# Position tables of an attention layer as one stationary square, made two items ahead, and a reordering of three engines' queues

## The chip, the cores and the metric

One core of a Trainium2 chip runs the whole kernel. The metric is the device time of one execution in microseconds (us). A profiled execution also gives its span, the time from its first to its last instruction.

## The reference

Four layers on x of shape 4 x 16 x 16 x 1024 (1024 tokens, 1024 channels), each behind a group norm (32 groups, over tokens and channels) and with a residual sum:

```python
x = x + L0(gn(x))   # lambda layer: q, k, v projections, position table, 4 heads
x = x + L1(gn(x))   # masked attention, 16 heads of 64, then Wo
x = x + L2(gn(x))   # attention, 16 heads of 64, biases, position tables, then a projection
x = x + L3(gn(x))   # 3x3 filter, tensor-train channel product (4 cores), bias, relu

# L2, for one image (H = W = 16) and one head of 64 channels
attn = (q * scale) @ k.T
rel_h = einsum('bhwc,hkc->bhwk', q, rel_pos_h[h - k + H - 1])
rel_w = einsum('bhwc,wkc->bhwk', q, rel_pos_w[w - k + W - 1])
attn = softmax(attn + rel_h[..., :, None] + rel_w[..., None, :])
out = attn @ v
```

## The kernel before

Channels lie on the partitions, tokens on the free axis. The five engines run queues written out by hand, tied together by semaphores; SyncE and ScalarE issue the DMAs. Every large product is made in three matmuls, since both operands are split into a rounded head (hi) and a rest (lo): hi x hi, lo x hi and hi x lo, summed in one bank of PSUM. Weights come from DRAM in slots of 4 chunks of 128 rows (w_load on SyncE), and GpSimd splits each (w_split, lines 226 and 228); three slots go round.

**Items.** Layers 1 and 2 are cut into 4 stages of 8 items (ITEMS = 32, PAIRS = 8). Stage s holds one layer (s = 0, 1: layer 1; 2, 3: layer 2) for one half of the tokens, two images; item i is one pair of heads, j = i % 8. Items 16 to 31 are layer 2's. With the last item of a stage done, 8 out blocks of 24 matmuls make the output projection (in item 8, 16, 24 for the stage before).

**TensorE's queue** in item i (attention_pe): scores(i) (line 1182), relative(i + 1) (line 1234), project K(i + 1), Q(i + 2) and V(i), 24 matmuls each (line 1138), attend(i - 1) (lines 1203, 1214). In items with j = 0 attend(i - 1) stands ahead of V(i), and the out blocks follow. Item 30 has K(31), V(30), attend(29), scores(31). The end mixes the halves of the last out blocks with V(31), attend(30), attend(31) and then with build_m, 16 pairs of matmuls that make the matrix M of layer 3; their heads are copied by ScalarE (line 1754), their rests by VectorE (line 1759), over two banks. last_pe (line 1786) waits for all of M.

**Position tables.** relative makes, per query and head, the products with all 31 entries of both tables: 24 matmuls with the queries stationary and 64 columns of table moving, into half a bank each of REL = (7, 0). Bank 7 is also Q's, bank 0 also V's, so relative waits for v_turned, that is turn_values (line 1497) on VectorE. ScalarE copies the result to SBUF in two parts (evac_relative, line 1387) and issues one DMA to DRAM (line 1624); SyncE reads it back with 8 DMAs whose skewed pattern picks each query's own entries (strips_from_dram, line 1636), and VectorE adds row and column part (sum_relative, line 1530).

**Softmax.** Per item 4 steps k: VectorE adds the tables and takes the maximum (lines 1470, 1473), ScalarE makes exponentials with their sum (line 1353), VectorE inverts (line 1488), ScalarE normalises (line 1363), VectorE turns 32x32 squares (line 1484). The turned probabilities and values go through DRAM; ScalarE copies the values (take_v, line 1344). ScalarE copies heads of Q, K and O (lines 1373/1377, 1396/1398, 1408/1410), VectorE makes their rests (1504/1506, 1513/1515, 1536/1539).

**Group norm of the next stage.** VectorE adds each out block to x (lines 1547, 1549), takes statistics (373), aggregates (379) and makes group moments (328 to 337), GpSimd the power (388), VectorE coefficients (342, 393). In items j = 1 to 4, chunk pairs are normalised: y on both engines (408, 406), head on ScalarE (414), rest on VectorE (419).

## Time and profile before

| | |
|---|---|
| times of the kernel before | 1235.68 us median of 3 (1235.05 to 1236.21) |
| the profiled execution | 1237.92 us, its span 1236.1 us |
| TensorE matmuls busy | 1198.9 us (97%) |
| VectorE, GpSimd, ScalarE busy | 697.4 (56%), 641.8 (52%), 475.7 (38%) |
| mean granted clock of TensorE | 0.99 of full speed |
| DMA | 171.81 MB, mean 139 GB/s |
| chain that ended last | TensorE 80%, VectorE 9%, issue 4%, ScalarE 3%, DMA 3% |

The busy time is the union of an engine's rows; matmuls overlap in their ends, so a mean duration of one (some 390 ns) is longer than the distance of two. Distances and counts tell the pace. The chain of waits is followed back from the last instruction to what released each step; a piece of it with "x72" is 72 instructions on end. Idle time of an engine that holds up nobody costs nothing.

### The profile page before, as it was taken

What the parts mean: (1) busy time and instruction counts of PE and PEld (TensorE: products, weight loads), DVE (VectorE), ACT (ScalarE), POOL (GpSimd) and SP (SyncE); (2) the same over time, 40 slices, a digit from 0 to 9 for tenths busy, and PEclk for the clock granted to TensorE, in tenths of its full rate; (3) what the DMA queues carried; (4) which work ended last, traced back from release to release, by engine and by line L of the source; (5) the groups of instructions that cost most, each with busy time, mean ns of one, the idle gap of its engine ahead of it and who ended that gap; (6) DMA issues with size and microseconds to landing.
All of it is one profiled execution on the core that took longest, in us unless ns stands there. A gap on an engine that the chain in (4) does not pass through costs nothing.

```text
span 1236.1 us, 19275 instructions
## 1 busy us (share of the span) xinstructions
PE 1198.9 (97%) x6640; PEld 970.9 (79%) x6640; DVE 697.4 (56%) x1434; ACT 475.7 (38%) x1229; POOL 641.8 (52%) x726
## 2 busy tenths in 40 slices
PE   6999999999999999999999999999998999999998
PEld 4788896478888888888878878788787878777887
DVE  7534443775665433765552577867337787458312
ACT  3611241035655410755540154545105545343312
POOL 4633389346556566656556645555564655463000
PEclk9999999999999999999999989999998999999999
DMA  5211114025666753576665357868535677720012
GB/s 186 84 44 51 35 52 122 8 65 178 189 187 180 208 167 95 151 206 178 198 181 158 96 157 211 237 197 242 174 103 161 176 209 229 208 97 1 34 35 68
DMA packets 159136, 171.81 MB, mean 139 GB/s; under 512 B 30656, under 2 KB 110176, under 8 KB 159040
## 3 DMA queue, kind: packets, MB, share of 16 engines
q1 hardware_dynamic: 148736, 163.70, 45.2%
q10 hardware_dynamic: 10304, 6.88, 1.8%
q8 instruction: 53, 0.87, 0.3%
q14 instruction: 43, 0.35, 0.1%
HBM read 120.20 MB, written 46.14 MB: 135 GB/s over the span
## 4 chain that ended last, share of the span: by engine, by line
PE 80%; DVE 9%; issue 4%; ACT 3%; DMA 3%; POOL 1%; SPq 1%; ACTq 0%; DVEq 0%; POOLq 0%
PE PS L1138 47%; PE PS L1786 7%; PE PS L682 7%; PE PS L962 3%; PE PS L1182 3%; PE PS L971 2%; PE PS L977 2%; PE PS L1214 2%; PE PS L1803 2%; PE PS L665 1%; PE PS L1203 1%; PE PS L1234 1%; DVE PS L1470 1%; DVE part L1530 1%; DVE bst L257 1%
## 5 line engine op out<-in xcount | busy, mean ns | idle before, releaser
L1138 PE MATMUL PS<-XB,w_hi 128*128 128x512 f32 x1024 | 334.6, 396 | 1.8 <-POOL w_lo L228 1.2
L226 POOL CAST w_hi<-w_raw 128x512 fp32r<-128x512 f32 x195 | 124.6, 639 | 298.6 <-PE PS L1138 214.8
L228 POOL TENSOR_TENSOR w_lo<-w_raw,w_hi 128x512 fp32r<-128x512 f32 x195 | 256.8, 1317 | 15.6
L1138 PEld LDWEIGHTS PS<-XB,w_hi 128*128 128x128 f32 x1024 | 194.0, 190 | 45.7 <-issue 3.2
L1353 ACT ACTIVATE part<-PS,nmax 128x256 f32<-128x256 f32 (+1 forms) x256 | 112.4, 444 | 290.7 <-DVE nmax L1473 182.4
L1138 PE MATMUL PS<-XB,w_lo 128*128 128x512 f32 x512 | 201.1, 393 | 0.0
L1138 PE MATMUL PS<-XB,part 128*128 128x512 f32 x768 | 189.0, 395 | 0.6 <-ACT part L1387 0.6
L1138 PEld LDWEIGHTS PS<-XB,part 128*128 128x128 f32 x768 | 145.5, 191 | 31.5 <-issue 1.0
L1484 DVE STREAM_TRANSPOSE part<-part 128x384 f32<-128x384 f32 (+1 forms) x128 | 82.1, 641 | 70.2 <-ACT part L1363 68.5
L1363 ACT ACTIVATE part<-part,prec 128x256 f32<-128x256 f32 (+1 forms) x256 | 105.9, 474 | 35.3 <-DVE prec L1488 27.2
L228 POOL TENSOR_TENSOR part<-part,part 128x512 fp32r<-128x512 f32 x85 | 111.2, 1309 | 6.8
L1138 PEld LDWEIGHTS PS<-XB,w_lo 128*128 128x128 f32 x512 | 97.1, 190 | 19.6 <-issue 0.2
L1138 PE MATMUL PS<-part,w_hi 128*128 128x512 f32 x344 | 111.0, 391 | 0.2 <-POOL w_lo L228 0.2
L226 POOL CAST part<-part 128x512 fp32r<-128x512 f32 x85 | 53.8, 633 | 102.5 <-PE PS L1138 95.6
L1138 PEld LDWEIGHTS PS<-part,w_hi 128*128 128x128 f32 x344 | 64.6, 188 | 14.6 <-issue 1.1
L682 PE MATMUL PS<-XB,w_hi 128*128 128x512 f32 x256 | 70.9, 392 | 0.0
L1138 PE MATMUL PS<-part,w_lo 128*128 128x512 f32 x172 | 66.9, 389 | 0.0
L1530 DVE TENSOR_TENSOR part<-part 128x512 f32<-128x512 f32 x64 | 61.2, 975 | 0.3 <-DMA part<-strips 0.3
L1138 PE MATMUL PS<-part,part 128*128 128x512 f32 x252 | 60.6, 389 | 0.0
L598 DVE COPY part<-PS 64x512 f32<-64x512 f32 x32 | 34.6, 1080 | 44.2 <-PE PS L700 43.9
L682 PEld LDWEIGHTS PS<-XB,w_hi 128*128 128x128 f32 x256 | 47.4, 188 | 9.4
L1138 PEld LDWEIGHTS PS<-part,part 128*128 128x128 f32 x252 | 47.1, 188 | 9.7
(135 smaller groups left out, 1800.7 us busy)
## 6 DMA issues: line engine op xcount, KB each, us to landing
w_raw<-in_w SPq DMA_DIRECT2D x187, 256.0 KB, 2.8
part<-in_w SPq DMA_DIRECT2D x85, 256.0 KB, 3.0
part<-turned SPq DMA_DIRECT2D x32, 512.0 KB, 5.5
turned<-part SPq DMA_DIRECT2D x60, 256.0 KB, 4.4
turned<-part SPq DMA_DIRECT2D x64, 192.0 KB, 3.4
part<-turned SPq DMA_DIRECT2D x32, 384.0 KB, 4.4
values<-part SPq DMA_DIRECT2D x128, 64.0 KB, 2.3
part<-values SPq DMA_DIRECT2D x32, 256.0 KB, 4.7
```

What stands on the lines that cost most here:

```text
L226: pool.tensor_copy(hi, raw).then_inc(w_hi_done, 1)
L228: pool.tensor_tensor(lo, raw, hi.bitcast(F32), ALU.subtract).then_inc(w_ready, 1)
L598: last = nc.vector.tensor_copy(dst, src)
L682: m = nc.tensor.matmul(PS[:, 2 * (n % 2) + h, :], wt[:, (c % 4) * P:(c % 4) * P + P], x_part(hl, h, c), start=c == k == 0, stop=c == CK - ...
L962: m = nc.tensor.matmul(bank[0:rows * SIDE, (x - x0) * w:(x - x0) * w + w], table, Qs[:, jp, x * N + SIDE * y0:x * N + SIDE * y1], start=jp ...
L1138: m = nc.tensor.matmul(PS[:, bank, :], wt[:, (c % 4) * P:(c % 4) * P + P], rhs(hl, c), start=c == k == 0, stop=c == CK - 1 and k == 2)
L1182: m = nc.tensor.matmul(PS[:, S + 2 * a + hh, at + lo:at + hi], x[rows, qs], y[rows, cols], start=k == 0, stop=k == 2)
L1353: last = nc.scalar.activation(prob[:, n % 2, at:at + hi - lo], PS[:, S + k, qt * N + lo:qt * N + hi], ACT.Exp, bias=nmax[:, k, qt:qt + 1], ...
L1363: last = nc.scalar.activation(p, p, ACT.Copy, scale=prec[:, k, qt:qt + 1])
L1484: nc.vector.transpose(dst, src).then_inc(t_done, 1)
L1530: nc.vector.tensor_tensor(both_rel[:, n % 2, :, :, :], of_row, of_col, ALU.add).then_inc(rel_sum, 1)
L1786: m = nc.tensor.matmul(PS[:, bank, :], x3(hl, b, c, tt * P), w[:, c, half * HALF:half * HALF + HALF], start=c == k == 0, stop=c == CK - 1 ...
```

## The change

- The tables' product has the table as the stationary square (2 tables x 2 heads x 32 rows, 128x128) and all 512 queries moving, reordered to image column, image and row: 3 matmuls into bank 7. It is made for item i + 2, behind the fifth chunk of V(i) (values_block).
- Its result is turned by one VectorE transpose of 32x32 squares (turn_relative), and ScalarE issues four DMAs for it at the end of its item. The reading pattern follows the new order.
- In layer 2, evac_q and rest_of_q of item i + 2 stand ahead of the last normalisation and the last turn.
- take_v stands ahead of the last exponentials in items with j = 0 and in item 30.
- Norm: statistics and aggregation of each out block right behind its sum; group moments at the end of item j = 1, coefficients in j = 2, chunks in j = 2 to 5; the rest is made by GpSimd. rest_of_o stands two steps later.
- The first half of out block 6 stands ahead of attend(31); M goes over four banks.

```diff
-            for o in {ITEMS - 2: (0,), ITEMS - 1: (1, 2, 3, 4, 5)}.get(i, ()):
+            for o in {ITEMS - 2: (0,), ITEMS - 1: (1, 2, 3, 4, 5, 6)}.get(i, ()):
...
-            take((3, "O", o), 2, "O", o, (1,) if o < 6 else range(2))
+            take((3, "O", o), 2, "O", o, (1,) if o < 7 else range(2))
...
-            def rest(self, t, c):
-                nc.vector.wait_ge(self.y_dve, CK * t + c + 1)
-                nc.vector.wait_ge(self.hi, CK * t + c + 1)
-                nc.vector.tensor_tensor(self.out(t, 1, c), self.ytmp[:, c % 2, :], self.out(t, 0, c).bitcast(F32),
-                                        ALU.subtract).then_inc(self.lo, 1)
+            def rest(self, eng, t, c):
+                eng.wait_ge(self.y_dve, CK * t + c + 1)
+                eng.wait_ge(self.hi, CK * t + c + 1)
+                eng.tensor_tensor(self.out(t, 1, c), self.ytmp[:, c % 2, :], self.out(t, 0, c).bitcast(F32),
+                                  ALU.subtract).then_inc(self.lo, 1)
...
-    all_rel = carve(19456, [P, 4, 2, 2, 32])
+    all_rel = carve(19456, [P, HALF])
...
-    REL = (X, 0)
...
-    LAST_OUT = (1, X, S, S + 1, S + 2, 0)
+    LAST_OUT = (1, X, S, S + 1, S + 2, 0, S + 3, S + 2)
...
     def out_bank(s, o):
-        return LAST_OUT[o % 6] if s == 3 else (O, 0)[o % 2]
...
-    M_AFTER = {(0, 1): (0, 1), (1, 1): (2, 3), (2, 1): (4,), (3, 1): (5, 6), (4, 1): (7, 8), (5, 1): (9,),
-               (6, 0): (10, 11), (6, 1): (12, 13), (7, 0): (14, 15), (7, 1): ()}
-    M_BANKS = (S + 3, O)
+        return LAST_OUT[o] if s == 3 else (O, 0)[o % 2]
...
+    M_AFTER = {(0, 1): (0,), (1, 1): (1,), (2, 1): (2,), (3, 1): (3, 4), (4, 1): (5, 6, 7), (5, 1): (8, 9),
+               (6, 1): (10, 11, 12), (7, 0): (13, 14, 15), (7, 1): ()}
+    M_BANKS = (O, 1, X, S)
...
-                        pe.wait_ge(rel_evac, 2 * (i - 1 - LO_KEYS) + 2)
+                        pe.wait_ge(rel_evac, i - LO_KEYS)
...
-                    if LO_KEYS <= i + 1 < ITEMS:
-                        pe.wait_ge(rel_evac, 2 * (i + 1 - LO_KEYS) + 2)
...
         def relative(i):
...
-            if i == ITEMS or layer_of(i) == 1:
...
+            if i >= ITEMS or layer_of(i) == 1:
...
-            pe.wait_ge(v_turned, i - 1)
-            if i % PAIRS == 2:
-                pe.wait_ge(sum_done, CK * (i // PAIRS))
...
-            for tt in range(4):
-                for k, (x, y) in enumerate(((qh[i % 2], rel_hi), (qh[i % 2], rel_lo), (ql[i % 2], rel_hi))):
-                    for hh in range(2):
-                        rows = slice(64 * hh, 64 * hh + 64)
-                        to = PS[:, REL[hh], 64 * tt:64 * tt + 64].rearrange("p (t n) -> p t n", t=2)
-                        m = nc.tensor.matmul(to, x[rows, tt * P:tt * P + P], y[rows, :, 32 * hh:32 * hh + 32],
-                                             start=k == 0, stop=k == 2)
-                        if (tt, k) == (3, 2):
-                            m.then_inc(rel_done, 1)
+            for k, (x, y) in enumerate(((rel_hi, qh[i % 2]), (rel_lo, qh[i % 2]), (rel_hi, ql[i % 2]))):
+                m = nc.tensor.matmul(PS[:, X, :], x.rearrange("p r n -> p (r n)"), y.rearrange("p (a y x) -> p y a x", a=2, y=SIDE),
+                                     start=k == 0, stop=k == 2)
+            m.then_inc(rel_done, 1)
...
         def out_block(s, o, chunks):
...
-                beside = 6 if s == 3 else 2
-                if c == 0 and o >= beside:
-                    pe.wait_ge(sum_done, CK * s + o - beside + 1)
+                if c == 0 and s < 3 and o >= 2:
+                    pe.wait_ge(sum_done, CK * s + o - 1)
+                if c == 0 and s == 3 and o == 7:
+                    pe.wait_ge(sum_done, CK * s + 5)
...
-                    pe.wait_ge(rel_evac, 2 * (ITEMS - LO_KEYS))
-                if s == 3 and c == 0 and 2 <= o < 5:
-                    pe.wait_ge(p_exp, 4 * LAST + o - 1)
+                    pe.wait_ge(rel_evac, ITEMS - LO_KEYS)
+                if s == 3 and c == 0 and out_bank(s, o) in range(S, S + 4) and o < 7:
+                    pe.wait_ge(p_exp, 4 * LAST + out_bank(s, o) - S + 1)
...
         def build_m(i):
...
-            if i == 1:
+            if i == 0:
...
-            if i >= 2:
-                pe.wait_ge(m_lo, i - 1)
+            if 1 <= i < 4:
+                pe.wait_ge(sum_done, 3 * CK + i)
+            if i >= 4:
+                pe.wait_ge(m_lo, i - 3)
...
         def score_block(i):
...
-            relative(i + 1)
...
+        def values_block(i):
...
+            project(i, "V", range(0, 5))
+            relative(i + 2)
+            project(i, "V", range(5, CK))
...
-                project(i, "V", range(CK))
+                values_block(i)
...
-                project(i, "V", range(CK))
+                values_block(i)
...
-        for o in (3, 4, 5):
+        for o in (3, 4, 5, 6):
...
-        for o in range(6):
-            out_block(3, o, range(4, CK))
-            for k in M_AFTER[o, 1]:
-                build_m(k)
-        for o in range(6, CK):
-            for half in range(2):
+        for o in range(CK):
+            for half in range(0 if o == 7 else 1, 2):
...
-                if i > LO_KEYS:
-                    act.wait_ge(rel_done, 2 * (i - LO_KEYS) - 2)
+                if i > LO_KEYS + 1:
+                    act.wait_ge(rel_done, i - LO_KEYS - 1)
...
-        def evac_relative(i):
-            if i == ITEMS or layer_of(i) == 1:
-                return
-            if i > LO_KEYS:
-                act.wait_ge(strips_out, 16 * (i - LO_KEYS))
-            for hh in range(2):
-                act.wait_ge(rel_done, 2 * (i - LO_KEYS) + hh + 1)
-                nc.scalar.activation(all_rel[:, :, :, hh, :],
-                                     PS[:, REL[hh], 0:4 * 64].rearrange("p (t a n) -> p t a n", t=4, a=2), ACT.Copy).then_inc(rel_evac, 1)
-            strips_to_dram(act, i)
...
-            evac_relative(i + 1)
...
-            if i == LAST:
+            early = i and j == 0 or i >= LAST - 1
+            if early:
...
+            if layer_of(i) == 2:
+                evac_q(i + 2)
...
-            if 0 < i < LAST:
+            if i and not early:
...
-            if 1 <= j <= 4:
-                for c in (2 * j - 2, 2 * j - 1):
+            if 2 <= j <= 5:
+                for c in (2 * j - 4, 2 * j - 3):
...
-                for c in (2 * j - 2, 2 * j - 1):
+                for c in (2 * j - 4, 2 * j - 3):
...
-            evac_q(i + 2)
+            if layer_of(i) == 1:
+                evac_q(i + 2)
...
+            if LO_KEYS <= i + 2 < ITEMS:
+                strips_to_dram(act, i + 2)
...
+        def turn_relative(i):
...
+            if i >= ITEMS or layer_of(i) == 1:
+                return
+            dve.wait_ge(rel_done, i - LO_KEYS + 1)
+            if i > LO_KEYS:
+                dve.wait_ge(strips_out, 64 * (i - LO_KEYS))
+            nc.vector.transpose(all_rel, PS[:, X, :]).then_inc(rel_evac, 1)
...
-        norm.group_stats(1)
...
-            if i >= 2 and j != 1:
-                rest_of_o(i - 2)
...
+            if i >= 2 and j != 1:
+                rest_of_o(i - 2)
...
+            if layer_of(i) == 2:
+                rest_of_q(i + 2)
...
-            if j == 1:
+            if j == 2:
...
-            if 1 <= j <= 4:
-                for c in (2 * j - 2, 2 * j - 1):
+            if 2 <= j <= 5:
+                for c in (2 * j - 4, 2 * j - 3):
...
-                for c in (2 * j - 2, 2 * j - 1):
-                    norm.rest(s + 1, c)
-            rest_of_q(i + 2)
+            if layer_of(i) == 1:
+                rest_of_q(i + 2)
...
-            sum_relative(i + 1, 1)
+            turn_relative(i + 2)
...
+            sum_relative(i + 1, 1)
...
-                    if o:
-                        stats_of(s - 1, o - 1)
-                stats_of(s - 1, CK - 1)
-                norm.aggregate(s + 1, range(CK), 16)
+                    stats_of(s - 1, o)
+                    norm.aggregate(s + 1, (o,), 2 * o + 2)
+            if j == 1:
...
-            if o >= 6:
+            if o == 7:
...
-                for k in (2 * o - 12, 2 * o - 11):
-                    stats_of(3, k)
...
-        for o in range(4, CK):
+            if o in (1, 2):
+                stats_of(3, o - 1)
+        for o in range(2, CK):
...
     def strips_to_dram(sp, i):
...
-        sp.wait_ge(rel_evac, 2 * done + 2)
-        whole = strips[buf].rearrange("(t p) n -> p t n", p=P)
-        sp.dma_start(whole, all_rel[:, :, :, :, :].rearrange("p t a b n -> p t (a b n)")).then_inc(strips_out, 16)
+        sp.wait_ge(rel_evac, done + 1)
+        rows = strips[buf].rearrange("(ax y) n -> ax y n", y=SIDE)
+        for b in range(4):
+            src = all_rel[32 * b:32 * b + 32, :].rearrange("p (y n) -> p y n", y=SIDE)
+            sp.dma_start(rows[:, :, 32 * b:32 * b + 32], src).then_inc(strips_out, 16)
...
     def strips_from_dram(sp, i):
...
-        sp.wait_ge(strips_out, 16 * (done + 1))
+        sp.wait_ge(strips_out, 64 * (done + 1))
...
-            at = buf * HALF * P + tt * P * P + 15
-            for k, first, steps in ((0, at - 8 * (tt % 2), (SIDE * P - 1, P)), (1, at + 64, (SIDE * P, P - 1))):
+            at = (buf * HALF + SIDE * SIDE * (tt // 2) + 8 * (tt % 2)) * P + 15
+            for k, first, steps in ((0, at - 8 * (tt % 2), (P - 1, SIDE * P)), (1, at + 64, (P, SIDE * P - 1))):
...
+            if n == PROBS_AT[LAST] + 2:
+                values_from_dram(sp, LAST)
...
-                values_from_dram(sp, LAST)
-            if n == PROBS_AT[LAST] + 2:
...
     def attention_pool(pool):
...
-                if n == (slots[(PAIRS * s + 3, "Q"), 0] if s else slots[(2, "Q"), 0]):
+                if n == slots[(PAIRS * s + 2, "K"), 0] + 8:
...
-            if n == slots[(ITEMS - 1, "Q"), 0]:
+                for j in range(2, 6):
+                    if n == slots[(PAIRS * s + j + 1, "K"), 0] + 8:
+                        for c in (2 * j - 4, 2 * j - 3):
+                            norm.rest(nc.gpsimd, s + 1, c)
+            if n == slots[(ITEMS - 1, "V"), 0]:
...
-            if n == slots[(3, "O", 3), 1]:
+            if n == slots[(3, "O", 6), 1]:
...
-            if n == slots[(3, "O", 5), 1]:
+            if n == slots[(3, "O", 7), 0]:
...
```

## Rows read from the trace of the kernel before

**Rows 1.** The chain of waits, one item of layer 2: start us, us, what.
```profile
832.88 1.62 PE PS L1182 x24
834.50 1.26 PE PS L1234 x24
835.76 16.52 PE PS L1138 x72
852.28 1.88 PE PS L1203 x16
```

**Rows 2.** TensorE's timeline: start, us, line, operation, [idle before, released by].
```profile
722.51 2.42 PE L1234 MATMUL PS<-part,part 64*128 64x64 f32 x24 [2.50 <-DVE part L1497]
...
791.65 1.53 PE L1234 MATMUL PS<-part,part 64*128 64x64 f32 x24 [1.70 <-DVE part L1497]
...
930.63 2.97 PE L1138 MATMUL PS<-XB,part 128*128 128x512 f32 x12 [0.59 <-ACT part L1387]
...
994.77 1.68 PE L1234 MATMUL PS<-part,part 64*128 64x64 f32 x24 [0.96 <-DVE part L1497]
```

**Rows 3.** Busy time of each engine, granted clock, DMA share by stretches.
```profile
696.30:743.70 47.40, 44.38 (x257) 36.10 (x256) 38.46 (x84) 24.39 (x67) 24.39 (x25) 0.93 0.50 139
...
1086.40:1121.50 35.10, 32.99 (x154) 26.40 (x152) 26.48 (x29) 19.00 (x17) 18.40 (x18) 1.00 0.15 46
```

**Rows 4.** The chain of waits, the projections behind two late tables blocks.
```profile
724.93 18.84 PE PS L1138 x72
...
996.45 17.92 PE PS L1138 x72
```

**Rows 5.** Timeline of TensorE and ScalarE, late attention products and a copy.
```profile
870.33 1.95 PE L1203 MATMUL PS<-part,part 128*64 128x256 f32 x16 [2.21 <-issue]
...
1053.70 3.42 PE L1203 MATMUL PS<-part,part 128*64 128x256 f32 x16 [2.21 <-issue]
...
869.62 0.62 ACT L1344 ACTIVATE part<-part 128x512 f32<-128x512 f32 x1
```

**Rows 6.** TensorE's timeline, the last attention product.
```profile
1085.39 1.08 PE L1203 MATMUL PS<-part,part 128*64 128x256 f32 x8 [0.85 <-DMA part<-turned]
```

**Rows 7.** The chain of waits, matmuls of layer 0.
```profile
196.92 20.60 PE PS L971 x48
217.52 6.87 PE PS L977 x16
```

**Rows 8.** Timeline of ScalarE and VectorE in the item of rows 1.
```profile
838.01 0.66 ACT L1387 ACTIVATE part<-PS 128x256 f32<-128x256 f32 x2
...
846.46 0.20 ACT L1353 ACTIVATION_READ_ACCUMULATOR part<-PS,nmax 128x1 f32 x1
...
849.57 0.75 DVE L1506 SCALAR_TENSOR_TENSOR part<-PS,bias,part 128x512 fp32r<-128x512 f32 x1 [0.33 <-ACT part L1377]
...
852.54 0.70 DVE L1497 STREAM_TRANSPOSE part<-PS 128x512 f32<-128x512 f32 x1
```

**Rows 9.** DMA of 832.88:854.16 and 846.2:849.9, stretch, SyncE's issue.
```profile
q10 hardware_dynamic: 528, 0.26, 4.1%
part<-values SPq DMA_DIRECT2D x1, 256.0 KB, 5.3
...
q1 hardware_dynamic: 861, 0.16, 21.2%
...
832.88:854.16 21.28, 21.28 (x138) 17.34 (x138) 15.34 (x24) 10.53 (x30) 12.49 (x13) 1.00 0.79 237
...
860.31 0.48 SPq L1672 DMA_DIRECT2D part<-values  x1
```

**Rows 10.** The page's costliest groups, a line's rows, GpSimd's timeline.
```profile
L228 POOL TENSOR_TENSOR w_lo<-w_raw,w_hi 128x512 fp32r<-128x512 f32 x195 | 256.8, 1317 | 15.6
...
L419 DVE TENSOR_TENSOR XB<-part,XB x40: 676/693/1765, 246.1 to 1012.0; 128x512 fp32r<-128x512 f32 x40
...
838.82 0.61 POOL L226 CAST part<-part 128x512 fp32r<-128x512 f32 x1 [5.04 <-PE PS L1138]
```

10 lines of the change are left out of this document (5 added, 5 removed).

## The prediction, made before the run

> **What bounds the kernel now.** I read the shares of busy time first: TensorE is busy for 97% of the span (table above), no other engine for more than 56%. So a microsecond counts only if TensorE's own row loses it: work taken off TensorE, or a pause of it. Next I read the chain of waits in a quiet item of layer 2 [rows 1]. Scores 1.62, position tables 1.26, three projections 16.52 and the attention product 1.88 follow each other without a pause, 21.28 us in all. The reader is to see that nothing but TensorE sets this item. I call the end of its scores T0 (834.50).
>
> Then I listed TensorE's rows that carry an idle time. Four tables blocks of layer 2 wait for VectorE's line 1497 (turn_values, which frees bank 0 of REL): 2.50, 1.70 and 0.96 us here, 2.50 once more at 947.76 [rows 2]. After such a wait the same work is slower: the mean granted clock of the stretch from 696 to 744 is 0.93 [rows 3], and the 72 projections behind take 18.84 and 17.92 us in place of 16.52 [rows 4]. A part of them runs at the lower level, 1.2 GHz, the rest at 2.4. Three attention products, at 870.33, at 1053.70 and a like one at 643.97, come 2.21 us late, marked "issue"; ScalarE's take_v (869.62 for 0.62 us) ends 0.1 us before the first of them starts, so that copy is the releaser [rows 5]. The last product waits 0.85 us for a DMA [rows 6].
>
> **The position tables.** Removed: 24 matmuls of 64 columns per item, 1.26 us [rows 1]. Added: 3 of 128x512. At 229 ns (16.52/72) they are 0.69 us; 16 items x 0.57 = 9.1 us. Their moving operand is read in runs of 16 elements, which no full-rate row here does. Lines 971 and 977 move 512 columns, one in runs of 4 elements and one contiguously, and both take 429 ns a matmul (20.60/48, 6.87/16) [rows 7]. So scattered reading is free there, and I take 229 ns. The bound the other way is 429 ns, 1.29 us per item and no gain: 9 us. A gain beyond 0.57 is excluded, since 229 ns is the fastest 512-column row.
>
> ScalarE loses two copies (line 1387, 838.01 for 0.66 us, with the issue behind it 1.1), VectorE gains one transpose like line 1497's, 0.70 us [rows 8]. It stands where VectorE would next wait for V, so the wait covers it; without that cover 0.70 would come off the 1.9 us of slack below.
>
> **Their place.** The block moves behind the fifth chunk of V and an item further ahead. It no longer waits for turn_values, since bank 0 is not used. What goes [rows 2, 4], against the quiet item: 2.50 + (2.42 - 1.26) + (18.84 - 16.52) = 5.98, twice; 0.96 + 0.42 + 1.40 = 2.78; 1.70 + 0.27 = 1.97. With the waits for line 1387 (0.59, and a like one of 0.52 at 705.37) that is 17.8 us. What is late next is the queries' rest (q_lo): the block stands 11.0 + 15 x 0.229 = 14.5 us after T0, and behind it the rest of V, the attention product and the next scores are queued. Before, line 1506 ended at 850.32, T0 + 15.8 [rows 8]: too late by 1.3. The change puts ScalarE's copy right behind the last exponential and VectorE's rest ahead of the last turn. That exponential ends at 846.66, T0 + 12.2 [rows 8]; without line 1387 ahead of it some 1.1 earlier, T0 + 11.1, just as the queries' product is done. Copy 0.67, rest 0.75: ready at T0 + 12.6, slack 1.9 us. After the out blocks VectorE today starts late because statistics and group moments stand ahead of the maxima; they are spread or moved behind the next item, so it starts about 1 us late, inside the slack. In the layer 1 items 14 and 15 no sum of tables stands ahead, and the old order already gives about T0 + 12.7.
>
> **DMAs of the move.** ScalarE issues 4 DMAs per item instead of 1, after turn_relative (about T0 + 17 to 19): about 0.5 us each by SyncE's issue in [rows 9], twice that if the queues are full (an estimate), 2 to 4 us. Queued behind them are evac_o and the next exponentials, due at about T0 + 21.5. So they are covered at the low end, and the high end takes some of the next item's slack. The bytes are the same but come in 2048 pieces of 128 bytes, against 528 packets now. These 528 took 4.1% of 16 engines over 21.28 us, 26 ns each; the strip reads of 192 bytes 14.6 ns (21.2% of 16 x 3.7 us / 861) [rows 9]. Between those prices the engines get 1.0 to 2.5 us more work each per item, on a share of 0.79 [rows 9]: 0.86 to 0.93. I take the lower, nearer in size. Weight loads have two slots of slack, so TensorE should not see it; the item in which it might is below. The page "DMA: Bandwidth & Descriptors" of the Trainium skill (Specifications) says that transfers below 512 bytes do a read-modify-write and miss line rate. That speaks against these pieces; 26 ns would then be no upper bound. The 192-byte rows here are reads, so no run shows it yet.
>
> **Take_v early.** In items 16, 24 and 30 the values' copy moves ahead of the last exponential. Gone: 3 x 2.21, and behind the last one 3.42 - 1.88 = 1.54 of slower products: 8.1 us [rows 1, 5]; 3.42 against 1.88 is near the ratio of the two levels. The copy needs the values in SBUF: issued at 860.31 (T0 of that item 855.78, so T0 + 4.5) and, at the 5.3 us that the like load took an item before, landing at T0 + 9.8 [rows 9], while the product can start at T0 + 11.0. The margin is 0.6 us after the copy. A load 2 us later would give back 1.4 each, 4 us.
>
> **Normalisation.** Two subtractions per item for four items of each stage go from VectorE to GpSimd (1.32 us each by its other subtractions, line 228). They stand in GpSimd's long pause during attention and scores (5.04 us before 838.82) [rows 10], so they cost nothing; without that pause 2.6 us would come off the some 3 us by which a split weight is ahead of its use. VectorE's subtraction takes 0.68 at least and up to 1.77 [rows 10]. The page "SBUF — State Buffer" (Who interferes with whom) says that a VectorE instruction with two SBUF inputs contends with a GpSimd one that reads SBUF, and one fully waits; by it two more GpSimd reads may hold VectorE for up to 2.6 us per such item and eat the 1.9 of slack. The spread of rows 10 agrees that there is something of the kind.
>
> **The end.** One more half block ahead of the last attention product covers its wait, 0.85 us [rows 6]; four banks instead of two for the M products, with their waits of about 0.5 each, are worth 1.3 us: after the last attention the phase took 35.1 us [rows 3], and laying products and copies out by hand gives 33.8, with TensorE waiting 1.8 us for VectorE's last copy. It may be worth nothing. Together 2.1. Charged: the last scores now come at T0 + 12.9 and need the keys' rest at T0 + 13.5, 0.6 us; item 30's product comes some 5 us sooner, its values' load only 3 to 4: 1.0 us.
>
> **Sum.** 9.1 + 17.8 + 8.1 + 2.1 - 1.6 = 35.5. The profiled execution took 1237.92 (span 1236.1), the median of the runs is 1235.68, 2.24 less; the saving applies to either. 1235.68 - 35.5 = 1200.2, so 1200.
>
> **Rivals.** (1) *Part is given back*: tables matmuls at 429 ns (9 us), or values that land late under the small pieces (4 to 8 us). For: no row shows either in its new form; against: [rows 7], and the margin of 0.6. 1209. (2) *The pauses after the out blocks stay*, as VectorE is still late there and another of its results is next; 12 us back: 1212, or 1217 with the other two. For: VectorE starts those items late today [rows 2]; against: the next result in line, the keys' rest, is made at about T0 + 14.5 and due at T0 + 19.1. (3) *Slower*: the queries' rest misses T0 + 14.5 in every item, so the block waits in the middle of V. A wait of 0.96 cost 2.78 and one of 2.50 cost 5.98 [rows 2, 4], as the clock falls too; 14 items at 2.5 us each eat the gain, which is decided at about 0.9 us beyond the slack. At the old place of line 1506 (1.3 late, some 3.5 each) it would be 1200 + 49 = 1249. Against: the two moves of this change. (4) *The change doesn't do what it says*: the waits move one for one, 1235.
>
> **Chances.** Forecast 0.62, with its own range 1192 to 1206; rival 1 0.20; rival 2 0.10; rival 3 0.06; rival 4 0.02. 1190 to 1214 leaves out rivals 3 and 4, the far end of 2 and a little of the forecast. About 0.2% is what a measurement of this kernel can tell from no change. Faster 0.92, same 0.02, slower 0.06.
>
> **What would show it.** Right: a steady item of 20.7 us; a tables block of 3 matmuls in about 0.7 us with no idle ahead; no row "issue 2.21" before attention; the granted clock 1.00 in the items after the out blocks. Wrong: idle before the tables block released by q_lo (rival 3); a block of 1.3 us (rival 1); VectorE as releaser of other TensorE rows after the out blocks (rival 2); line 1344 waiting for a DMA in items 16 and 24.

## The result, and the profile after

The changed kernel takes 1201.9 us (median of 4 runs, 1201.2 to 1204.8) against 1236.0 for the kernel before on the same chip: ratio 0.972, 95% interval 0.969 to 0.975. The forecast was 1200, with a range of 1190 to 1214. Unaltered and run five times more on another chip it gave 1202.9 (0.971, 0.969 to 0.974). The nine runs together have a median of 1202.2; "the changed kernel" is that number below. The profiled execution took 1204.8, span 1202.8.

The page of the kernel after: busy time by engine, then packets and queues.

```profile
PE 1178.2 (98%) x6304; PEld 949.5 (79%) x6304; DVE 674.2 (56%) x1418; ACT 462.9 (38%) x1197; POOL 683.4 (57%) x758
...
DMA packets 184478, 171.78 MB, mean 143 GB/s; under 512 B 64192, under 2 KB 135520, under 8 KB 184384
...
q10 hardware_dynamic: 35648, 6.89, 3.0%
```

TensorE is still the bound. The packets under 512 bytes have doubled (30,656 before), while ScalarE's queue, q10, takes 3.0% of the engines' time.

The chain of waits of the kernel after, a quiet item (start, us, what), which answers [rows 1]:

```profile
712.66 1.62 PE PS L1179 x24
714.28 14.50 PE PS L1137 x63
728.78 0.72 PE PS L1227 x3
729.50 2.06 PE PS L1137 x9
731.57 1.88 PE PS L1200 x16
733.45 1.62 PE PS L1179 x23
```

One item is 20.79 us against 21.28. The tables block is 0.72 in place of 1.26, and V in its two parts takes 0.04 more. The block stands in the middle of V with nothing idle ahead of it.

The same kernel by windows (length, then busy us of each engine, granted clock, DMA share, GB/s): the stretch that answers the first of [rows 3], and the phase of the M products behind the last attention.

```profile
691.87:733.45 41.58, 41.58 (x233) 33.11 (x232) 33.51 (x65) 21.18 (x59) 26.79 (x27) 1.00 0.61 172
1056.50:1088.16 31.66, 30.25 (x142) 24.90 (x140) 25.52 (x29) 18.27 (x17) 17.91 (x17) 0.97 0.15 42
```

The clock is 1.00 where it was 0.93. What is left of TensorE's pauses is this (timeline of PE from 600 us on, its rows with an idle time; in brackets the idle time ahead and what ended it):

```profile
851.66 1.95 PE L1200 MATMUL PS<-part,part 128*64 128x256 f32 x16 [1.56 <-issue]
1023.04 1.70 PE L1179 MATMUL PS<-part,part 64*128 64x256 f32 x24 [0.96 <-DVE part L1504]
1038.96 1.30 PE L1200 MATMUL PS<-part,part 128*64 128x256 f32 x10 [0.40 <-issue]
1054.88 1.69 PE L1200 MATMUL PS<-part,part 128*64 128x256 f32 x8 [1.84 <-DMA part<-turned]
1083.78 0.50 PE L1267 MATMUL PS<-ttA,part 96*128 96x256 f32 x2 [0.28 <-DVE part L1763]
1088.16 2.11 PE L1790 MATMUL PS<-part,XB 128*128 128x512 f32 x8 [1.13 <-DVE part L1763]
```

Every wait of [rows 2] is gone. Of the three of [rows 5], those of items 16 and 30 are gone and 1.56 of item 24's 2.21 is left. Three stand near the end: the keys' rest ahead of scores(31) (0.96), the values ahead of attend(30) (0.40) and the last probabilities ahead of attend(31, 1) (1.84, before 0.85 [rows 6]).

The starts of the scores say where the 33.3 us between the two profiled spans lie: 24.4 in items 17 to 23 and 25 to 29, 4.3 in item 16, 1.2 in item 24, 4.0 in item 30 and 0.2 before all these, less 0.7 behind scores(31).

ScalarE's and VectorE's timeline in another quiet item, whose scores end (T0) at 818.21:

```profile
829.35 0.69 ACT L1372 ACTIVATE part<-PS,bias 128x512 fp32r<-128x512 f32 x1 [1.37 <-PE PS L1137]
...
830.08 0.75 DVE L1495 SCALAR_TENSOR_TENSOR part<-PS,bias,part 128x512 fp32r<-128x512 f32 x1 [1.90 <-ACT part L1372]
```

The queries' rest is ready at 830.83, T0 + 12.6; the block starts at T0 + 14.3. Both are as forecast. The total, the item and this step agree, and so it looked as if the whole sum were right. The experiments say that it isn't.

### The profile page after: what moved, and what is told of

Same layout as the page of the kernel before. It is cut to its first block, busy times and chain, and to the rows that moved or that the text cites. A ratio compares the mean times of both kernels' runs of the same rounds, so it can differ in the third digit from the quotient of the medians.

```text
span 1202.8 us, 18617 instructions
## 1 busy us (share of the span) xinstructions
PE 1178.2 (98%) x6304; PEld 949.5 (79%) x6304; DVE 674.2 (56%) x1418; ACT 462.9 (38%) x1197; POOL 683.4 (57%) x758
## 4 chain that ended last, share of the span: by engine, by line
PE 91%; DVE 4%; DMA 2%; issue 1%; SPq 1%; POOL 1%; ACT 0%; ACTq 0%; POOLq 0%; DVEq 0%
PE PS L1137 55%; PE PS L1790 7%; PE PS L682 7%; PE PS L1179 4%; PE PS L962 3%; PE PS L971 2%; PE PS L977 2%; PE PS L1200 2%; PE PS L1211 2%; PE PS L1807 2%; PE PS L665 1%; DVE part L1763 1%; PE PS L1227 1%; DVE bst L257 1%; PE PS L700 1%
## 5 line engine op out<-in xcount | busy, mean ns | idle before, releaser
L1179 PE MATMUL PS<-part,part 64*128 64x256 f32 (+1 forms) x768 | 53.0, 284 | 1.0 <-DVE part L1504 1.0
```

Source lines behind the costliest of these rows:

```text
L1179: m = nc.tensor.matmul(PS[:, S + 2 * a + hh, at + lo:at + hi], x[rows, qs], y[rows, cols], start=k == 0, stop=k == 2)
```

## The experiments

Times are medians; the difference is to the changed kernel's 1202.2. The number in brackets is the ratio to the kernel before, measured beside it on the same chip, with its 95% interval.

### Which part brought what: four kernels between before and after

The first undoes the whole of the tables and leaves the rest of the change. (REL is bank X and bank 0 again; relative(), evac_relative() and the strips' layout are those of the kernel before.)

```
         def score_block(i):
             scores(i, 0)
             scores(i, 1)
+            relative(i + 1)
...
-            project(i, "V", range(0, 5))
-            relative(i + 2)
-            project(i, "V", range(5, CK))
+            project(i, "V", range(CK))
...
-            if layer_of(i) == 2:
-                evac_q(i + 2)
             normalize(i, 3)
```

> The changed kernel with the whole of the tables undone: 24 matmuls of 64 columns one item ahead behind the scores, two ScalarE copies, one DMA of the strips, the queries' copy and rest late. Everything else of the change stays (statistics and moments spread, the normalisation's rests on GpSimd, take_v early, four banks for M, the order at the end). Prediction's sum: tables 9.1 + their place 17.8 = 26.9 slower than the changed kernel, 1229. Rival: the spread statistics and moments alone let VectorE's turn_values come sooner behind the out blocks, so the waits of 2.50, 1.70 and 0.96 are gone without a new place, and the tables are worth only 9 to 15 us: 1211 to 1217.

Measured: 1209.0 (0.977, 0.974 to 0.979), 6.8 slower, not 27. On TensorE's timeline no tables block waits for turn_values any more, although the block is at its old place, in its old banks and behind the same wait. The block of item 18 follows its scores at once, where [rows 2] have 2.50 us:

```profile
713.28 1.69 PE L1182 MATMUL PS<-part,part 64*128 64x256 f32 x24
714.81 1.42 PE L1234 MATMUL PS<-part,part 64*128 64x64 f32 x24
```

The rival came true, and below its own low end. Next, the statistics alone are undone, once with the new tables and once with the old ones.

```
-            if j == 2:
+            if j == 1:
                 norm.coefficients(s + 1)
-            if 2 <= j <= 5:
-                for c in (2 * j - 4, 2 * j - 3):
+            if 1 <= j <= 4:
+                for c in (2 * j - 2, 2 * j - 1):
...
                     add_out(s - 1, o)
-                    stats_of(s - 1, o)
-                    norm.aggregate(s + 1, (o,), 2 * o + 2)
-            if j == 1:
+                    if o:
+                        stats_of(s - 1, o - 1)
+                stats_of(s - 1, CK - 1)
+                norm.aggregate(s + 1, range(CK), 16)
                 norm.group_stats(s + 1)
```

> The changed kernel with the statistics undone: after each stage's out blocks VectorE makes the statistics in one row behind the sums, with the group moments ahead of the next item's maxima, and the next normalisation stands in items 1 to 4 of a stage, not 2 to 5. Tables stay as changed. If two remedies are each enough for the waits of 2.50, 1.70 and 0.96 us (the tables' new bank and place, and VectorE's lighter item), the waits stay away here too: at most 3 us slower than the changed kernel, 1202 to 1206. If the light items are needed: VectorE comes some 2 us later into the queries' rest of item 17 and 25, past the 1.9 us of slack, and the tables block waits there: 5 to 12 us slower.

> The kernel with both undone: tables, their place and the queries' copies as before, statistics and normalisation as before; kept are only the rests on GpSimd, the rest of the attention output and the last sum of tables one step later in VectorE's row, take_v early, four banks for M and the order at the end. If the statistics' spread alone had removed the waits that the prediction gave to the tables' place: they are back here, 2.50 twice, 1.70, 0.96, 12 to 18 us slower than with old tables alone (1209), so 1221 to 1227. If instead the two late steps or GpSimd's rests removed them: 1209 to 1213, without the waits.

Measured: 1205.1 with the new tables (0.973, 0.971 to 0.975), 1215.9 with the old ones (0.982, 0.980 to 0.984). With the new tables there are two small waits, 0.61 ahead of item 17's block and 0.60 ahead of item 25's; these items are 0.8 and 0.9 us longer. With the old ones two of the four waits are back, both at 1.32. So with the new tables the statistics matter little (2.9 us, at the edge of "each is enough"). The second result lies between its two theories: the waits came back, but at half their size and at half of their places. A third thing had shortened them as well. The last kernel takes the normalisation's lower parts from GpSimd too:

```
                 for c in (2 * j - 2, 2 * j - 1):
                     norm.y(nc.vector, s + 1, c)
+                for c in (2 * j - 2, 2 * j - 1):
+                    norm.rest(nc.vector, s + 1, c)
```

> The kernel with tables and statistics as before (1215.9, waits of 1.32 at two tables blocks) and, on top, the lower parts of the normalisation on VectorE again. What is left of the change is the sum of tables and the rest of the attention output one step later in VectorE's row, take_v early, four banks for M and the order at the end. Theory: GpSimd's rests, 2 of 0.7 us in items 1 to 4 of a stage, are what shortened the waits for turn_values; then they are 1.85 twice (2.50 less the 0.65 us of the sum that now stands behind), 1.0 and 0.3 us, with the slower products behind them 8 to 12 us in all: 1224 to 1228. Rival: the order of VectorE's row is what did it: the waits of 1.70 and 0.96 stay away, those of 1.32 stay under 1.6, and the time is under 1219.

Measured: 1219.9 (0.986, 0.984 to 0.989). TensorE's rows that wait for VectorE in the stretch of items 17 to 29, first with the rests on GpSimd, then on VectorE:

```profile
717.05 1.53 PE L1234 MATMUL PS<-part,part 64*128 64x64 f32 x24 [1.32 <-DVE part L1500]
...
933.46 1.53 PE L1234 MATMUL PS<-part,part 64*128 64x64 f32 x24 [1.32 <-DVE part L1500]
```

```profile
717.90 2.59 PE L1234 MATMUL PS<-part,part 64*128 64x64 f32 x24 [1.90 <-DVE part L1500]
...
938.51 1.53 PE L1234 MATMUL PS<-part,part 64*128 64x64 f32 x24 [1.91 <-DVE part L1500]
1004.53 1.53 PE L1234 MATMUL PS<-part,part 64*128 64x64 f32 x24 [0.31 <-DVE part L1500]
```

The waits are those that the theory named (1.85 twice, 0.3), its time was 4 us too high: 1.0 of wait did not come back, and the slower products behind a wait were dearer in my estimate than here. What is left between this kernel and the one before is two instructions one step later in VectorE's row (the second sum of tables, the rest of the attention output), take_v early, the banks for M and the order at the end.

The ladder, read off the starts of the scores in the five traces. "Twelve items" is from scores(17) to scores(24) and from scores(25) to scores(30); item 24 holds the out blocks.

| kernel | median | twelve items | step | item 24 |
|---|---|---|---|---|
| before | 1236 to 1238 | 273.85 | | 67.36 |
| VectorE's two late steps, take_v, end | 1219.9 | 267.14 | 6.7 | 65.02 |
| + rests on GpSimd | 1215.9 | 261.82 | 5.3 | 65.02 |
| + statistics spread | 1209.0 | 255.36 | 6.5 | 65.02 |
| + tables, place, early queries (changed) | 1202.9 | 249.43 | 5.9 | 68.36 |

The last row is the second profile of the changed kernel. In the first one item 24 takes 66.17, and 64.53 in kernels with the new tables in which it has no wait, so its wait costs 1.6 to 3.8 us where it stands.

The twelve items hold no early take_v and none of the end, so the first step is what VectorE's two late steps bring; it is taken by difference and was not tried alone. Three steps on VectorE's row bring 18.5 us, and the last one 5.9, which is 12 times the 0.50 by which the block became shorter. With the old tables and the light row of VectorE no pause is left in the twelve items, so the new place has nothing to remove there. (Place and block were undone together, neither alone.) With the heavy row, the statistics undone, it has: the new tables are worth 10.8 us there (1215.9 - 1205.1), 4 more.

### Are the early queries needed?

```
-            if layer_of(i) == 2:
-                evac_q(i + 2)
             normalize(i, 3)
...
-            if layer_of(i) == 1:
-                evac_q(i + 2)
+            evac_q(i + 2)
```

and the like for rest_of_q in VectorE's row.

> The changed kernel with one thing undone: in layer 2 ScalarE's copy of the queries stands behind the normalisation of the last probabilities, the keys, take_v and the next stage's normalisation again, and VectorE's rest of the queries behind the last turn, the keys' rest and normalisation. The prediction's rival 3 said: every item 1.3 us late at the tables block, some 3.5 each, 49 us in all, so 1249 us. Worked out anew from the trace after the change: in a quiet item the queries' rest would be ready at T0 + 13.7 (last exponential 827.98, then 1.0 + 0.6 + 0.6 + 0.7 + 0.75, T0 818.21), 0.8 ahead of the block at T0 + 14.5, so no wait; in the eight items of layer 2 that carry a quarter of the next normalisation ScalarE has four more instructions ahead and VectorE two, 2 to 2.5 us, so a wait of 1 to 2 us there, at two to three times its own length with the clock: 8 x 2 to 3.5 = 16 to 28 us, 1218 to 1230. A third theory, that the early queries are not needed: within 0.2% of the changed kernel, 1202.

Measured: 1222.8 (0.989, 0.985 to 0.993), 20.6 slower, inside the second theory's range. Its chain of waits around one of the eight items:

```profile
754.12 0.61 ACT XB L414
754.74 0.58 ACT part L1372
755.32 0.88 issue
756.20 0.96 PE PS L1227 x3
757.16 2.06 PE PS L1137 x9
759.22 1.88 PE PS L1200 x16
```

The queries' copy (L1372) stands behind the normalisation's head (L414), and TensorE waits for the copy. The waits are 2.76, 1.52, 1.51 and 1.52 in items 18 to 21, and the same again in 26 to 29: 14.6 us. An item with one takes 22.55 us (738.48 to 761.03), 1.76 more than without: the wait of 1.52 and 0.24 in the block. Those waits cost hardly more than their length, but the two of 2.76 cost 4.5 and 3.0 us (item 18 takes 25.32, item 26 23.81). Over the twelve items it is 18.9 us. So the early queries do not earn anything by themselves; they are what the new place asks for, at a price of 20 us if it isn't paid.

### Take_v

```
-            early = i and j == 0 or i >= LAST - 1
+            early = i == LAST
```

> The changed kernel with take_v of items 16, 24 and 30 behind the last exponential, the queries' and keys' copies again (only in the last item it stays early). Theory: each of the three attention products waits for it; against the changed kernel, in which item 16 and 30 wait 0 and 0.40 and item 24 waits 1.56, they wait 2.2 to 3 each, so 5 us of waits and some 1.5 of slower products behind them: 5 to 7 us slower, 1207 to 1209. Rival, that the values' landing sets the end of the wait in item 24 and not ScalarE's order: then item 24 waits 2.2 or less in both, and the loss is 4 us or less.

Measured: 1208.5 (0.976, 0.973 to 0.979), 6.3 slower, as the theory had it for the time.

```profile
643.15 1.60 PE L1211 MATMUL PS<-part,part 128*64 128x128 f32 x32 [2.71 <-issue]
...
855.62 1.95 PE L1200 MATMUL PS<-part,part 128*64 128x256 f32 x16 [2.71 <-issue]
...
1026.35 1.95 PE L1200 MATMUL PS<-part,part 128*64 128x256 f32 x16 [2.21 <-issue]
```

Items 16 and 24 wait 2.71 where they waited 2.21 before, for the queries' copy now stands ahead of take_v as well. The starts of the scores tell what this costs. Item 16 takes 66.98 us against 64.22. Item 24 takes 67.30, between the changed kernel's 66.17 and 68.36: there the early copy starts as soon as the values have landed (850.91, copy at 850.93), so their load sets the end of the wait, while the late one starts 2.1 us after the landing (852.83, copy at 854.90). The rival has a point there. Item 30 takes 16.87 against 15.63, since scores(31) do not wait for the keys' rest any more. The waits of 0.40 and 1.84 that stood behind are gone too. So item 16 pays in full, item 30 in part and item 24 not surely. This profiled execution is the fastest of its four (1206.3, only 1.5 above that of the changed kernel); the rest of the 6.3 is not seen in it.

### The rests on GpSimd, in the changed kernel

```
             if 2 <= j <= 5:
                 for c in (2 * j - 4, 2 * j - 3):
                     norm.y(nc.vector, s + 1, c)
+                for c in (2 * j - 4, 2 * j - 3):
+                    norm.rest(nc.vector, s + 1, c)
```

> The changed kernel with the lower parts of the next stage's normalisation on VectorE again, behind its own halves, in place of GpSimd; 2 subtractions of about 0.7 us in each of 16 items. Theory that the move to GpSimd is worth nothing here, as VectorE's rest of the queries is ahead of them and what is behind them has 2 us of slack: within 0.2% of the changed kernel. Rival: VectorE's turn_relative and turn_values come 1.4 us later, the values' write and load follow, and the attention products wait: 4 to 10 us slower. Other rival, that two GpSimd reads hold VectorE back more than its own two subtractions would: up to 2 us faster, and its instructions of line 1519 shorter than 1.77 at the worst.

Measured: 1205.1 (0.974, 0.970 to 0.977), runs 1201.9 to 1206.2; 2.9 slower, with runs that overlap. Its profiled execution is the shortest of its four (span 1200.1): item 24's wait is missing, and in item 30 a new one stands ahead of attend(29) while that ahead of scores(31) has grown from 0.96 to 1.78.

```profile
1020.46 1.95 PE L1200 MATMUL PS<-part,part 128*64 128x256 f32 x16 [1.64 <-issue]
1024.18 1.70 PE L1179 MATMUL PS<-part,part 64*128 64x256 f32 x24 [1.78 <-DVE part L1504]
```

What leads to them is in ScalarE's timeline: the strips are stored only once turn_relative is done, here at 1007.82, and the attention output's copy and the exponentials are queued behind.

```profile
1007.85 3.49 ACTq L1626 DMA_DIRECT2D strips<-part  x4
1011.39 0.69 ACT L1394 ACTIVATE part<-PS,bias 128x512 fp32r<-128x512 f32 x1 [7.17 <-issue]
```

In the changed kernel that copy starts at 1009.76. So the same move that was worth 4.0 us under a heavy row (1219.9 to 1215.9) is worth less where other steps have already lightened it.

### The price of the block

```
-            for k, (x, y) in enumerate(((rel_hi, qh[i % 2]), (rel_lo, qh[i % 2]), (rel_hi, ql[i % 2]))):
+            for k, (x, y) in 2 * list(enumerate(((rel_hi, qh[i % 2]), (rel_lo, qh[i % 2]), (rel_hi, ql[i % 2])))):
```

> The changed kernel with the three matmuls of the position tables issued twice in each of the 16 items of layer 2 (the sum restarts, the values are the same). Theory: nothing covers the block, so 16 x 0.70 = 11.2 us slower, 1213, and the block takes 1.4. Were a part of the block hidden (by loads of weights or a wait behind it), less than 8. Were TensorE at the edge of a wait for the second half of V's weights, more than 14.

Measured: 1211.9 (0.980, 0.977 to 0.982), 9.7 slower.

```profile
731.32 1.60 PE L1227 MATMUL PS<-part,part 128*128 128x512 f32 x6
```

Each item takes 21.54 us in its trace, 0.75 more. Over 16 items that is 12.0; the profile lacks item 24's wait, worth 1.6 to 3.8 us where it stands, so this and the 9.7 agree as far as these runs tell. Nothing covers the block: a matmul of 512 columns read in runs of 16 costs TensorE 0.24 to 0.25 us here, one of the projections 0.23.

### One DMA in place of four

```
-        rows = strips[buf].rearrange("(ax y) n -> ax y n", y=SIDE)
-        for b in range(4):
-            src = all_rel[32 * b:32 * b + 32, :].rearrange("p (y n) -> p y n", y=SIDE)
-            sp.dma_start(rows[:, :, 32 * b:32 * b + 32], src).then_inc(strips_out, 16)
+        to = bass.AP(strips.tensor, buf * HALF * P, [[32, 4], [SIDE * P, 32], [P, SIDE], [1, 32]])
+        sp.dma_start(to, all_rel.rearrange("p (y n) -> p y n", y=SIDE)).then_inc(strips_out, 64)
```

> The changed kernel with the strips stored by one DMA per item with the same 2048 pieces in place of four. Theory: ScalarE's 3.5 to 4.4 us of issues per item are hidden in nearly every item, so no more than 1 us of gain, within 0.2%. If the issue goes by instruction, it takes 0.6 to 1 us and the copy of line 1394 behind it stands ahead of the scores' end; if it goes by pieces, it takes 2 to 4 us as before. Rival: the four issues delay the first exponentials and SyncE's own issues (5.59 us for four stores in item 24): 2 to 5 us faster.

Measured: 1247.2 (1.007, 1.005 to 1.010), 45 us slower than the changed kernel, which nothing of mine foresaw. The issue did get short, 0.55 us. ScalarE's store, then SyncE's row up to the read of the same strips:

```profile
812.05 0.55 ACTq L1622 DMA_DIRECT2D strips<-part  x1
```

```profile
826.15 0.42 SPq L212 DMA_DIRECT2D part<-in_w  x1
826.62 0.43 SPq L212 DMA_DIRECT2D w_raw<-in_w  x1
831.84 4.98 SPq L1634 DMA_DIRECT2D part<-strips  x8
```

SyncE stops at 827.05 until 831.84 for the strips: the one store of 2048 pieces landed 19.8 us after its issue (in an item in which SyncE did not have to wait, at most 17.7), while each of the four stores of 512 pieces landed within 4.9 us (median of 64; 6.6 at most). Behind SyncE's read are the weight loads, behind these GpSimd's split, and behind that TensorE:

```profile
853.05 0.77 PE L1137 MATMUL PS<-XB,w_hi 128*128 128x512 f32 x1 [5.37 <-POOL w_lo L228]
```

The pieces are as many and as large as in the changed kernel, so their number alone is not the cause. But the edit changes two things: there is one DMA in place of four, and the outermost dimension of its pattern in DRAM is 4, where each of the four has 32. The queue's packets differ too. Of ScalarE's queue (packets, MB, share of 16 engines), first the one store (window 813 to 832), then the four stores of one item of the changed kernel (815 to 823):

```profile
q10 hardware_dynamic: 2052, 0.26, 9.3%
```

```profile
q10 hardware_dynamic: 2112, 0.26, 21.2%
```

A store has a few packets more than it has pieces: 16 in the kernel before (528 for 512 [rows 9]), 16 in each of the four (2112 for 2048), 4 in the one. In the trace the four extra packets of the store issued at 648.30 end 11.3, 12.5, 14.5 and 20.0 us after its issue, as four separate streams would. So the one store may have been spread over 4 of the 16 engines only, each shared with the loads of the other queue. That is an inference; the record does not name a packet's engine.

Nor is the time per piece a fixed one. Over the 16 stores of this kernel the last packet ended 9.3 to 20.0 us after the issue. The shortest is the one issued at 890.82, beside the out blocks, and for 1.4 us (893.4 to 894.8) its packets alone are on the queues:

```profile
q10 hardware_dynamic: 577, 0.07, 34.9%
```

That is 2.4 ns a piece, against 9.7 for the 19.8 us above. What is shown is that this store is 45 us dearer than the four. Whether one DMA as such is, or its pattern, was not tried; a single store whose pattern begins with 32 or more would tell.

### The end, and a version to beat both

```
             exps(i, 2)
+            if i == LAST - 1:
+                evac_k(i + 1)
             normalize(i, 2)
...
+            if i == LAST - 1:
+                rest_of_k(i + 1)
...
+                probs_to_dram(sp, LAST, 1)
                 values_from_dram(sp, LAST)
-                probs_to_dram(sp, LAST, 1)
```

> The changed kernel unaltered, on the chip of the three runs beside it. 1202 us; its waits ahead of TensorE in items 24, 30 and 31 (1.56, 0.96, 0.40, 1.84 us in the first profile) tell which of them stand in every execution: by the theory the keys' rest and the last probabilities do (they come from an order), the one of item 24 does not (a queue's delay).

Measured: 1202.9, as given above. All four waits stand again in its profile: 2.14 in item 24, 0.90, 0.29 and 1.03. That bears the theory out for the keys' rest and the last probabilities; item 24's wait, which was to come and go, came again.

> The changed kernel with two orders altered near the end: ScalarE's and VectorE's parts of the last keys stand two steps sooner in item 30, and SyncE stores the last probabilities ahead of the last values' load. Theory: the waits are set by those orders, so 0.96 goes, of 1.84 at least 1.5 goes with some 0.9 of slower products behind it: 2.8 to 3.5 us faster than the changed kernel, 1199. Rival: another result is next in line at each place (probabilities' turn in item 30, the read back of the probabilities at the end): less than 1 us.

Measured: 1200.8 (0.971, 0.968 to 0.973; runs 1199.4 to 1203.8) beside 1202.9 for the changed kernel on the same chip: 2.1 less, with runs that overlap, so a lead that isn't sure. With the two orders altered, the wait for the keys' rest is gone and 1.03 became 0.29, for the read back of the probabilities. But the values are next in line: attend(30) waits 1.18 in place of 0.29. Here item 24 does not wait.

```profile
1036.95 1.95 PE L1200 MATMUL PS<-part,part 128*64 128x256 f32 x16 [1.18 <-issue]
...
1051.34 1.08 PE L1200 MATMUL PS<-part,part 128*64 128x256 f32 x8 [0.29 <-DMA part<-turned]
```

ScalarE's copy ahead of it waits until the values land at 1036.20 and starts at 1036.22. So both waits came from an order, and the rival was right as well: of the 2.22 us of waits 1.47 are left. The 2.1 us of the medians are not explained by this alone; item 24's missing wait may be a part of them. A further version loads item 23's values sooner and moves the M products a step:

```
-                if i < LAST and n == BACK_AT[i]:
+                if i < LAST and n == (PROBS_AT if i == 3 * PAIRS - 1 else BACK_AT)[i]:
                     values_to_dram(sp, i)
...
-               (6, 1): (10, 11, 12), (7, 0): (13, 14, 15), (7, 1): ()}
+               (6, 1): (11, 12, 13), (7, 0): (14, 15), (7, 1): ()}
```

> The version of the end (keys' rest of item 31 sooner, the last probabilities' store ahead of the last values' load) with two more orders: the values of item 23 are stored right behind its probabilities, ahead of two weight loads, and the M products stand one step sooner. Theory: the wait of 1.56 to 2.14 in item 24 hangs on the values' load at T0 + 8.1, which comes 1.7 sooner; with the slower product behind it 2 to 3 us in the executions that have it, and 0.5 to 1.1 before the last products: 1197 to 1199. Rival: the item 24 wait moves to the weights, which are loaded later, and the M copies only wait elsewhere: 1201, as the end's version.

Measured: 1202.3 (0.971, 0.969 to 0.973), no better than the end alone. Item 24 waits 2.41, attend(30) 1.49 and the last product 1.12.

```profile
833.15 5.74 SPq L1653 DMA_DIRECT2D turned<-part  x4
...
845.47 0.61 SPq L1677 DMA_DIRECT2D part<-values  x1
```

```profile
851.87 0.63 ACT L1339 ACTIVATE part<-part 128x512 f32<-128x512 f32 x1 [4.38 <-DMA part<-values]
```

The load went out 1.2 us sooner than in the changed kernel's second profile (846.63) and landed 0.7 later: about 6.4 us on the way, against 4.5. My theory, that SyncE's order sets this wait, fell: with the load sooner, the landing was not. The two edits were made together, and nothing shows that the M step gains.

What stays open is what makes item 24 wait in some executions only. In the five profiles of kernels with the new tables, four small stores and take_v early that have such a wait (1.16 to 2.41 us), SyncE took 3.7 to 5.7 us to issue the four stores of item 23's probabilities, with ScalarE's four small stores issued beside them. In the three without a wait it took 3.0 to 3.1, here in the kernel of the end:

```profile
832.40 3.05 SPq L1653 DMA_DIRECT2D turned<-part  x4
```

That goes together; which causes which was not tried. The kernel with the old tables, which has one store in place of four, does not wait there (65.02 us for the item in the table, 68.36 in the changed kernel).

## Why the prediction was right, and where it was not

The total was right: 1202 against 1200, in the range. The sum behind it was not, and its largest term was put to the wrong edit. That the total came out all the same is in part luck: the pauses went by edits that the sum had at nothing.

- **What bounds the kernel**: right. Each wait or matmul that an undoing put into TensorE's row made the kernel longer.
- **The position tables, 9.1**: right in mechanism. A matmul took 240 ns (0.72/3), near the 229 assumed, the item fell by 0.50 and not by 0.57, 8.0 in 16 items. The bound of 429 ns fell.
- **Their place, 17.8**: this is the step that failed. I wrote that the block "no longer waits for turn_values, since bank 0 is not used" and booked all of the waits of [rows 2] to it. True as a sentence, and the size of the pauses was right; but the same change made turn_values itself come in time, by three steps, and these brought 18.5 us in the twelve items without any new place. In each of them I had looked only for a cost: the statistics' spread came up as a slack of 1 us, the normalisation's rests "cost nothing", the sum of tables and the rest of the attention output that now stand one step later in VectorE's row were not priced at all. I asked of the removed wait what is late next, and did not ask of the other edits which of them would have removed it anyway. Given the rest of the change, the place is worth about 0 by the traces; with the statistics undone, 4 us.
- **q_lo at T0 + 12.6 with a slack of 1.9**: the time right to 0.1 us, the slack 1.7. Rival 3's place was right and its size too large. Undone, the wait comes in 8 items (and 0.17 in two more) and not in all, and costs 20.6 us and not 49. The trace of before could not say that: evac_relative() stood ahead of these steps in it, and I moved their time by 1.1 for the forecast and not for the rival.
- **Four DMAs on ScalarE, 2 to 4 us, covered**: covered as forecast, but 3.5 to 5.3 us in the changed kernel's two profiles, partly above the high end (in item 24 2.7 and 3.0). In the quiet item above evac_o() started at 818.61, just behind them, and the first exponential at 819.20, 0.2 after its maximum was ready. The small pieces take 12.8 ns each of an engine's time (9.8% of 16 engines in 20.79 us, 2549 packets), less than my lower price of 14.6. The "DMA: Bandwidth & Descriptors" page of the Trainium skill (Specifications) has transfers under 512 bytes slowed down by a read-modify-write; these are writes of 128 bytes. By the byte they do cost about twice as much as the kernel before's packets of 512 bytes (0.10 against 0.05 ns), which agrees with the loss of rate; a read-modify-write can't be told from the trace. The one DMA tried in their place was far dearer.
- **Take_v early, 8.1**: 6.3 measured by undoing it. Against the kernel before the 2.21 of items 16 and 30 is gone, and the slower product with it; but part of item 30's gain returns as the keys' wait below. Item 24 kept 1.2 to 2.4 us in most profiles, since the values' load went out at T0 + 8.1 and not at T0 + 4.5. That is rival 1's second half, at one item of three: 1.6 to 3.8 us (66.17 and 68.36 against 64.53 without a wait) in place of 4 to 8.
- **Normalisation on GpSimd, 0**: by itself 2.9 us in the changed kernel (unclear within its runs), 4.0 under the heavy row; VectorE is what it relieved. The "SBUF — State Buffer" page of the Trainium skill (Who interferes with whom) would have had GpSimd's reads hold VectorE up instead; the kernel without them is not faster.
- **The end, 2.1 - 1.6**: the M phase took 31.7 us, 32.4 before without the half block that moved, so 0.7 of the 1.3. The keys' rest cost 0.96 (forecast 0.6), the values of item 30 0.40 (1.0). The wait of [rows 6] was to go and went from 0.85 to 1.84: the change also moved SyncE's load of the last values ahead of the last probabilities' store, a queue that I had not walked through. The store went out at 1043.59, 1.9 after the turn that it needs.

So the forecast was right by a sum that two views of one saving both would have given: the pauses went, whichever edit took them. The rival "the pauses after the out blocks stay" had the right engine in view, VectorE, and the wrong sign for what the change does to it.

## What to carry to other kernels

When several edits of one change each could remove the same wait, count the wait once and say which edits are enough alone; only undoing them one at a time tells, and the saving of one depends on whether the others stand. Every edit that shortens the row of an engine behind which the bounding engine waits has a gain to be priced, not only a cost to be hidden. Where one DMA is to replace several, read when it lands and how many packets it has, and not only how long its issue takes. And walk each queue through in order where a change swaps two of its transfers.

## What the runs showed of the hardware

One DMA of 2048 pieces of 128 bytes, with 4 as the outermost dimension of its pattern, had 4 packets more than pieces and landed 9.3 to 20.0 us after its issue; four DMAs of 512 such pieces, with 32 outermost, had 16 more each and landed in 4.9 us each (median, 6.6 at most). Alone on the queues the one moved a piece in 2.4 ns, and in 9.7 on average over its 19.8 us beside the weight loads. Its issue was 0.55 us, that of the four 2.7 to 5.3. An operand read in runs of 16 elements cost a matmul of 512 columns at most 0.02 us (0.24 to 0.25 against 0.23).
